# Two edge-maximum layers of a graph network: the attribute product and the gathered rows are summed in PSUM, and the maximum scan runs in four pieces

## The reference, cut to what matters

```
hv = x @ W_in + b_in
for W, b in ((W_u0, b_u0), (W_u1, b_u1)):
    m = concatenate([hv[src], he], axis=-1)     # he: 64 attributes of each edge
    m = relu(m @ W + b)
    msg = segment_max(m, dst)
    hv = where(has_in, msg + hv, hv)
out = relu(hv @ W_ro + b_ro)
```

## Time and profile before

| | |
|---|---|
| device time, median of 3 runs | 6830.46 us |
| the three runs | 6829.79, 6830.46, 6848.0 us |
| span of the profiled execution (one core) | 6822.1 us |
| mean granted TensorE clock over the span | 0.765 of full speed |
| TensorE busy over the span | 70% |
| VectorE busy over the span | 49% |
| GpSimd busy over the span | 48% |

### The profile page before, as it was taken

The page is one execution under the profiler, slowest core; times in us unless marked ns, Lnnn a source line. Parts: engine busy times, 40 slices in busy tenths (PEclk is TensorE's granted clock), DMA queues, the critical chain, the costliest instruction groups (busy, mean ns, idle before and its releaser), DMA issues. The chain is left out here.

```text
span 6822.1 us, 83340 instructions
## 1 busy us (share of the span) xinstructions
PE 4796.2 (70%) x21859; PEld 3705.9 (54%) x21860; DVE 3317.7 (49%) x8140; ACT 1583.2 (23%) x4023; POOL 3256.3 (48%) x2940
## 2 busy tenths in 40 slices
PE   3666576999844438699959566466567877688868
PEld 2666455677433326477759434244445666566645
DVE  5544467323433337622331466588434555355554
ACT  1000075333100008300014222265221111111121
POOL 2666677777566648300020444564325555555510
PEclk8555588999866769899969655598677777777778
DMA  4888655000288856376646344486436776577710
GB/s 131 271 265 272 189 191 168 8 1 1 62 279 283 276 191 235 120 250 219 195 158 211 113 139 138 148 311 232 138 119 176 203 200 196 158 202 202 204 61 24
DMA packets 751400, 1183.52 MB, mean 173 GB/s; under 512 B 100921, under 2 KB 528682, under 8 KB 750982
## 3 DMA queue, kind: packets, MB, share of 16 engines
q1 hardware_dynamic: 366758, 553.94, 26.0%
q0 software_dynamic: 135904, 356.79, 18.8%
q10 hardware_dynamic: 248448, 269.39, 11.7%
HBM read 818.22 MB, written 361.10 MB: 173 GB/s over the span
## 5 line engine op out<-in xcount | busy, mean ns | idle before, releaser
L2452 POOL DMA_INDIRECT max_rows<-tab,src_r x784 | 743.0, 948 | 607.1 <-DVE msg L2546 292.0
L403 POOL DMA_INDIRECT counts<-put_n,put_at x400 | 565.6, 1414 | 212.6 <-issue 134.8
L1009 POOL DMA_INDIRECT late_rows<-tab,src_a x416 | 418.4, 1006 | 317.7 <-DMA slot_rows<-late_rows 177.5
L2546 DVE TENSOR_TENSOR msg<-max_rows,ps_e 128x512 f32<-128x512 f32 x392 | 265.8, 687 | 557.3 <-PE ps_e L2483 158.2
L986 PE MATMUL ps_b<-q,sel_t 128*128 x832 | 277.8, 499 | 367.1 <-DVE sel_t L905 251.4
L707 POOL DMA_INDIRECT logit_rows<-tab,src_a x416 | 416.9, 1002 | 247.9 <-DVE logits L927 136.0
L707 POOL DMA_INDIRECT logit_rows<-tab_kv,src_a x416 | 396.8, 954 | 284.7 <-issue 125.1
L2483 PE MATMUL ps_e<-w,att 64*128 64x256 f32 x1568 | 515.1, 482 | 24.6 <-DMA att<-in_attr_t 17.2
L2558 DVE TENSOR_TENSOR_SCAN run<-same,run,ps_t 128x512 f32<-128x512 bf16 x392 | 479.4, 1265 | 9.8 <-remote 5.5
L2527 ACT ACTIVATE back<-ps_b 128x512 f32<-128x512 f32 x392 | 222.4, 596 | 1094.4 <-PE ps_b L2504 463.3
L826 PE MATMUL ps_a<-msg,sel 128*128 128x264 f32 (+1 forms) x1664 | 412.8, 397 | 90.2 <-DVEq L758 46.7
(11 more groups left out here) (482 smaller groups left out, 9786.7 us busy)
## 6 DMA issues: line engine op xcount, KB each, us to landing
blocks<-counts SPq DMA_DIRECT2D x390, 320.0 KB
slot_rows<-logit_rows ACTq DMA_DIRECT2D x208, 512.0 KB
edge_rows<-slot_rows SPq DMA_DIRECT2D x208, 512.0 KB
seg_rows<-back ACTq DMA_DIRECT2D x196, 512.0 KB
slot_rows<-late_rows SPq DMA_DIRECT2D x104, 512.0 KB
sum_rows<-slot_rows SPq DMA_DIRECT2D x104, 512.0 KB
counts<-zeros ACTq DMA_DIRECT2D x130, 320.0 KB
wf<-in_L_ffn_W SPq DMA_DIRECT2D x57, 512.0 KB
```

What stands on the lines that cost most here:

```text
L403: nc.gpsimd.indirect_dma_start(out=g.counts, out_offset=bass.IndirectOffsetOnAxis(ap=g.put_at[:, j:j + 1], axis=0), in_=g.put_n[:, j:j + 1 ...
L1009: self.nc.gpsimd.indirect_dma_start(out=self.rows[:, b * Q + j, :], out_offset=None, in_=self.g.tab, in_offset=bass.IndirectOffsetOnAxis(a ...
L2452: nc.gpsimd.indirect_dma_start(out=rows[:, b * Q + j, :], out_offset=None, in_=table, in_offset=bass.IndirectOffsetOnAxis(ap=g.src_r[:, n ...
L2546: v.tensor_tensor(msg[:, s:s + 2, :], rows[:, s:s + 2, :], ps_e[:, k, :].rearrange("p (j d) -> p j d", j=2), ALU.add).then_inc(mixed, 1)
```

## The change

In `edge_max` alone, and in one more host layout of the attributes:

- `att` of a group is one tile of 128 partitions: the attributes of the first 256 edges on partitions 0 to 63, those of the last 256 on 64 to 127. `w` is loaded twice, onto both halves of the partitions.
- `edges(n)` makes the product the other way around: `w` is stationary (64 rows by 128 features), `att` moves (256 edges), so features stand on partitions at once. Four products, two on each half of the array's rows, in turn, straight into `ps_t`.
- `turn(n)` no longer transposes `msg`: it multiplies each gathered 128x128 block (stationary) by the float32 identity (moving), as a product and not as a transpose, and accumulates onto what `edges` left in `ps_t`.
- `mix(n)`, `msg` and `ps_e` are gone. `ps_t` has a ring of three groups (`R`) in place of two.
- `scan(n)` is four scans of 256 columns in place of two of 512.
- GpSimd's gather of group n waits for turn(n-4) in place of mix(n-4), SP's load of `att` for edges(n-4).

```diff
--- before.py
+++ after.py
@@ -2423,31 +2423,31 @@
 def edge_max(nc, g, table, w_dram):
...
+    R = 3
+    HG = GP // 2
     with Phase(nc) as ph:
         sb, ps, sem = ph.sb, ph.ps, ph.sem
         rows = sb("max_rows", [P, W, D], F32)
-        w = sb("w", [EA, D], F32)
-        att = sb("att", [EA, W, P], F32)
+        w = sb("w", [2 * EA, D], F32)
+        att = sb("att", [2 * EA, Q, HG], F32)
         same = sb("same", [P, Q, GP], BF16)
-        msg = sb("msg", [P, W, D], F32)
         run = sb("run", [P, Q, KD, GP], F32)
         back = sb("back", [P, W, D], F32)
-        ps_e = ps("ps_e", [P, 2, 512])
-        ps_t = ps("ps_t", [P, 2, KD, 512])
+        ps_t = ps("ps_t", [P, R, 2, 512])
         ps_b = ps("ps_b", [P, 2, 512])
...
-                        pool.wait_ge(mixed, 2 * (n - Q) + 2)
+                        pool.wait_ge(turned, 2 * (n - Q) + 2)
...
-                sp.dma_start(w[:], w_dram).then_inc(w_in, 16)
+                for h in range(2):
+                    sp.dma_start(w[h * EA:(h + 1) * EA, :], w_dram).then_inc(w_in, 16)
                 for n in range(RG):
                     b = n % Q
                     if n >= Q:
-                        sp.wait_ge(made, 2 * (n - Q) + 2)
-                    sp.dma_start(att[:, b * Q:(b + 1) * Q, :], g.ins["attr_t"][n * Q:(n + 1) * Q, :, :].rearrange("r e l -> e r l")
-                                 ).then_inc(att_in[b], 16)
+                        sp.wait_ge(made, n - Q + 1)
+                    sp.dma_start(att[:, b, :], g.ins["attr_g"][n]).then_inc(att_in[b], 16)
                     if n >= Q:
-                        sp.wait_ge(ran, 2 * (n - Q) + 2)
+                        sp.wait_ge(ran, 4 * (n - Q) + 4)
                     sp.dma_start(same[:, b, :], g.same_rows[n * GP:(n + 1) * GP].partition_broadcast(P)).then_inc(same_in[b], 16)
...
                 def edges(n):
                     b = n % Q
                     pe.wait_ge(att_in[b], 16 * (n // Q) + 16)
-                    for k in range(2):
-                        if n:
-                            pe.wait_ge(mixed, 2 * (n - 1) + k + 1)
-                        for j in range(2):
-                            ins = t.matmul(ps_e[:, k, j * D:(j + 1) * D], att[:, b * Q + 2 * k + j, :], w[:], start=True, stop=True)
-                        ins.then_inc(made, 1)
+                    if n >= R:
+                        pe.wait_ge(ran, 4 * (n - R) + 4)
+                    for c in range(KD):
+                        for h in range(2):
+                            at = slice(h * EA, (h + 1) * EA)
+                            ins = t.matmul(ps_t[:, n % R, h, c * HG:(c + 1) * HG], w[at, c * P:(c + 1) * P], att[at, b, :], start=c == 0, stop=False)
+                    ins.then_inc(made, 1)
 
                 def turn(n):
                     b = n % Q
-                    if n >= 2:
-                        pe.wait_ge(ran, 2 * (n - 2) + 2)
-                    pe.wait_ge(mixed, 2 * n + 2)
-                    for c in range(KD):
-                        for j in range(Q):
-                            ins = t.transpose(ps_t[:, n % 2, c, j * P:(j + 1) * P], msg[:, b * Q + j, c * P:(c + 1) * P], g.ident[:])
+                    pe.wait_ge(got[b], 64 * (n // Q) + 64)
+                    for h in range(2):
+                        for c in range(KD):
+                            for j in range(2):
+                                at = c * HG + j * P
+                                ins = t.matmul(ps_t[:, n % R, h, at:at + P], rows[:, b * Q + 2 * h + j, c * P:(c + 1) * P], g.ident[:],
+                                               start=False, stop=c == KD - 1 and j == 1)
                         ins.then_inc(turned, 1)
...
                 def give_back(n):
                     b = n % Q
-                    pe.wait_ge(ran, 2 * n + 2)
+                    pe.wait_ge(ran, 4 * n + 4)
...
-                def mix(n):
-                    b = n % Q
-                    dve.wait_ge(got[b], 64 * (n // Q) + 64)
-                    if n >= Q:
-                        dve.wait_ge(turned, KD * (n - Q) + KD)
-                    for k in range(2):
-                        dve.wait_ge(made, 2 * n + k + 1)
-                        s = b * Q + 2 * k
-                        v.tensor_tensor(msg[:, s:s + 2, :], rows[:, s:s + 2, :],
-                                        ps_e[:, k, :].rearrange("p (j d) -> p j d", j=2), ALU.add).then_inc(mixed, 1)
-
                 def scan(n):
                     b = n % Q
                     dve.wait_ge(same_in[b], 16 * (n // Q) + 16)
                     if n >= Q:
                         dve.wait_ge(returned, 2 * (n - Q) + 2)
+                    dve.wait_ge(turned, 2 * n + 1)
                     for c in range(KD):
-                        dve.wait_ge(turned, KD * n + c + 1)
                         if n:
-                            dve.wait_ge(ran, KD * (n - 1) + c + 1)
-                        v.tensor_tensor_scan(run[:, b, c, :], same[:, b, :], ps_t[:, n % 2, c, :], run[:, (b - 1) % Q, c, GP - 1:GP],
-                                             ALU.mult, ALU.max).then_inc(ran, 1)
+                            dve.wait_ge(ran, 4 * (n - 1) + 2 + c + 1)
+                        v.tensor_tensor_scan(run[:, b, c, 0:HG], same[:, b, 0:HG], ps_t[:, n % R, 0, c * HG:(c + 1) * HG],
+                                             run[:, (b - 1) % Q, c, GP - 1:GP], ALU.mult, ALU.max).then_inc(ran, 1)
+                    dve.wait_ge(turned, 2 * n + 2)
+                    for c in range(KD):
+                        dve.wait_ge(ran, 4 * n + c + 1)
+                        v.tensor_tensor_scan(run[:, b, c, HG:GP], same[:, b, HG:GP], ps_t[:, n % R, 1, c * HG:(c + 1) * HG],
+                                             run[:, b, c, HG - 1:HG], ALU.mult, ALU.max).then_inc(ran, 1)
...
                 v.memset(run[:, Q - 1, :, :], 0.0).then_inc(zeroed, 1)
                 dve.wait_ge(zeroed, 1)
-                mix(0)
-                mix(1)
                 for n in range(RG):
                     scan(n)
-                    if n + 2 < RG:
-                        mix(n + 2)
 
...
+    ap["attr_g"] = ap["attr_t"].reshape(RG, 2, 2, EA, P).transpose(0, 1, 3, 2, 4).reshape(RG, 2 * EA, 2 * P)
```

More of the change, by code:

```diff
@@ L2441, in edge_max @@
         stored = [sem(f"stored{b}") for b in range(Q)]
-        w_in, zeroed, made, mixed, turned, ran, returned, taken = (sem(x) for x in (
-            "w_in", "zeroed", "made", "mixed", "turned", "ran", "returned", "taken"))
+        w_in, zeroed, made, turned, ran, returned, taken = (sem(x) for x in (
+            "w_in", "zeroed", "made", "turned", "ran", "returned", "taken"))
         with nc.Block() as block:
@@ L2462, in _ @@
                     if n >= Q:
-                        sp.wait_ge(made, 2 * (n - Q) + 2)
-                    sp.dma_start(att[:, b * Q:(b + 1) * Q, :], g.ins["attr_t"][n * Q:(n + 1) * Q, :, :].rearrange("r e l -> e r l")
-                                 ).then_inc(att_in[b], 16)
+                        sp.wait_ge(made, n - Q + 1)
+                    sp.dma_start(att[:, b, :], g.ins["attr_g"][n]).then_inc(att_in[b], 16)
                     if n >= Q:
-                        sp.wait_ge(ran, 2 * (n - Q) + 2)
+                        sp.wait_ge(ran, 4 * (n - Q) + 4)
                     sp.dma_start(same[:, b, :], g.same_rows[n * GP:(n + 1) * GP].partition_broadcast(P)).then_inc(same_in[b], 16)
-                sp.wait_ge(w_in, 16)
+                sp.wait_ge(w_in, 32)
             @block.tensor
@@ L2473, in _ @@
                 t = nc.tensor
-                pe.wait_ge(w_in, 16)
+                pe.wait_ge(w_in, 32)
                 def edges(n):
```

## The result

The changed kernel took 6715.37 us (median of four runs, 6708.18 to 6723.0), the kernel before 6831.03 us in the same rounds. The ratio is 0.9825, with a 95% interval from 0.9809 to 0.984. The profiled execution has a span of 6706.4 us, against 6822.1 us.

What follows compares the result with a forecast made beforehand. TensorE's chain at a changing clock plus stops was taken to bound edge_max (6.44 us a group). At 5.3 us a group 223 us, plus 20 behind the last gathers, go from 6822.1: 6579 us span, 6587 us median, range 6520 to 6910.

Steps and rivals of the forecast that it cites:

- The step that failed: In edge_max, a group without stops at full clock takes its largest term; 5.3 us taken in place of 6.44, saving 223 us.
- Rival 1: In edge_max, the clock rises but TensorE's stops stay: 4.82 + 1.37 = 6.19 us a group, 6761 us; chance 0.11.
- The argument against rival 1: From 3580 to 3785 us TensorE works 205 us in 205 us, so heavy product work alone brings no stops.
- the argument for the clock: Long stages of float32 products had clock 0.93 to 1.00; with two of three steps products, edge_max should reach 0.93 or more.
- GpSimd's floor of 4.95 us: GpSimd's time for a group's gathers in edge_max without waiting, gaps between gathers included: 4.95 us.
- The term for the DMA engines: DMA packets of an edge_max group, 4.77 us, need 5.54 us at a share of 0.86, 4.77 at 1.
- The 5.3 us: Forecast time of an edge_max group, taken between GpSimd's 4.95 and the DMA engines' 5.54 us.
- The price of edges: TensorE's eight edges records cost 1.92 us at full clock, as before; 0.96 at the least if the halves run side by side.
- The side sentence on the Trainium skill: By the skill's up to 2x, edges would take 0.96 us and TensorE's full-clock sum 3.86 us, leaving the forecast unmoved.
- Rival 3: In edge_max, the clock goes on alternating but the halves overlap: 6.44 to 6.76 us a group, 6830 to 6893 us; chance 0.14.
- scans of 256 columns: VectorE's four scans a group take 0.73 us each, 2.9 us together, hidden behind TensorE.
- The tail: Work behind each edge_max call's last gather falls from 19.3 to 9.5 us, saving 10 us a call, 20 in all.

Runs made afterwards that it cites:

- eight groups of room: The changed kernel with eight groups of gathered rows in the buffer in place of four: 6702.09 us, ratio 0.9874 to the kernel before.
- two groups ahead: The changed kernel with GpSimd gathering group n only after TensorE has turned group n-2 (n-4 before): 6702.33 us, ratio 0.988.
- three groups ahead: The changed kernel with GpSimd gathering at most three groups ahead of TensorE's turn in place of four: 6656.81 us, ratio 0.9809.
- clearing in between: The changed kernel with GpSimd clearing a 128x256 tile that nobody reads after every two gathers: 6678.44 us, ratio 0.9837.
- turn as transposes: The changed kernel with turn as eight transposes for sixteen product records, overwriting the attribute products: 6654.21 us, ratio 0.9806.
- The run without stops: The kernel before with GpSimd's gathers replaced by plain transfers of the same bytes from fixed rows: 6270.63 us, ratio 0.9243.

## Why the prediction was wrong

**The step that failed** is "At full clock without stops the group takes the largest of GpSimd's 4.95, TensorE's 4.82 and DMA". The stops were written down as a cost of 1.37 us with no known cause, and the forecast let them go together with the half clock. The clock did rise, to 0.90, and the stops stayed: 5.93 us a group in place of 5.3. (5.93 - 5.3) x 196 = 123 us, which is nearly all of the 127 us between 243 and 116. Rival 1, "The clock rises but the stops stay", was the right mechanism at a chance of 0.11, and gave 6761 us, 46 us too slow. That it came so near is in part luck, since both its terms were off and in opposite directions: TensorE needs 3.88 us in place of 4.82, and what the gathers add is 5.93 - 3.88 = 2.05 us in place of 1.37. The measured time lies inside the stated range, which the rivals had made wide.

**The argument against rival 1 failed too.** The stretch with 205 us of work in 205 us shows no stop, but GpSimd does nothing in it (0.00). It spoke of products and the stops belong to gathers. The row had both numbers. The same rows hold a stretch that the argument for the clock passed over, 2300 to 2490 us, with gathers, 80.56 us of TensorE's work in 190 us, and 0.68.

**GpSimd's floor of 4.95 us** was right as its own pace (1.25 us a gather: in the changed kernel eight follow each other at that) and wrong as a bound of the group. In the stretches around 5430 us seven kernels needed 1.46 to 1.50 us for each gather:

| kernel | gathers, time | us each |
|---|---|---|
| changed | 8 in 11.87 | 1.48 |
| eight groups of room | 8 in 11.75 | 1.47 |
| two groups ahead | 12 in 17.72 | 1.48 |
| three groups ahead | 8 in 11.71 | 1.46 |
| clearing in between | 8 in 11.80 | 1.48 |
| turn as transposes | 12 in 17.48 | 1.46 |
| three gathers a group | 9 in 13.49 | 1.50 |

From the first to the last gather of the first call it is 1.45 (transposes) to 1.49 us (three gathers), and 1.53 us with two groups ahead. Six of the seven have four gathers in a group and could not tell a cost of each gather from a cost of each group; the one with three can, with 4.50 us a group. Four gathers make 5.9 us. The kernel before was over that, at 6.44, most likely for its loop through VectorE; the change took it down to the pace of the gathers, where it stops paying.

**The term for the DMA engines**, 4.77 to 5.54 us, was no bound either: with plain transfers of the same bytes a group took 3.87 us at a share of 0.90. The gathers' own packets were never tried at that pace. The 5.3 us stood between two bounds of which neither held.

**The price of edges** was taken in full, 1.92 us. The halves overlap and it is 1.07 us. The side sentence on the Trainium skill ("TensorEngine Tiling (Array Packing)", Theoretical Speedup: up to 2x for a contraction of 64 or less) gave the better sum: 3.86 us by it, 3.88 measured with plain transfers; 4.82 in the prediction. That the two agree to 0.02 us is luck in part, since edges came out 0.11 us dearer than by the page's factor and turn 0.07 us cheaper than its row. The speedup of eight records is 1.99 / 1.14 = 1.75.

**Rival 3** ("the same, but the halves overlap") had this sum, 3.86 to 4.10, and its sentence that work only goes from VectorE to TensorE is what the runs with plain transfers show: 0.9254 and 0.9243. For the kernel as it is it was wrong, since the clock did not go on alternating at 0.75 and the group fell from 6.44 to 5.93.

**The clock.** "Two steps of three are products" was given as the reason for 0.93 or more. It was 0.90, and the kernel before, with its transposes, had 0.94 without stops. So the transposes alone did not bring 0.75; it took the stops as well. With stops the work did count: 0.92 with products in turn, 0.81 with transposes. The rule of the Trainium skill ("TensorE: Matmul & The Clock Gate", Part 4) that the full clock does not engage for transposes is not settled by this. The run without stops had 0.94 with transposes in 1.94 of each 3.86 us, but products filled the rest, as in the last 16 us of the call.

**Right:** scans of 256 columns (0.729 and 0.723 us; 0.73 predicted); turn's sixteen records at 1.95 us; the DMA bytes at nothing (a run with an eighth of the gathered bytes took the same time). That the third `ps_t` group is worth nothing no run shows. **The tail** went from 19.3 us to 5733.67 - 5717.85 = 15.8 us behind the last gather, not to 9.5: 3.5 us in place of 10 in the first call. Its landing of 4 us stood on no row; the last gather's packets ended at 5720.40, 2.6 us behind it, so what was mis-sized is the work after the landing, 13.2 us in place of 5.6. The rows:

```profile
5716.90 0.95 POOL L2452 DMA_INDIRECT max_rows<-tab,src_r  x1 [0.30 <-issue]
```

and the last store:

```profile
5733.30 0.37 ACTq L2531 DMA_DIRECT2D seg_rows<-back  x1
```

**What stays open** is why indirect transfers of GpSimd hold this stage to 1.47 us each. It is not GpSimd alone: the first 16 gathers of a call start 1.25 us apart with nothing between. It is not bytes, room, the wait of GpSimd, late rows, or one of the other transfers. Whether the indirect form or the scattered rows do it was not tried. That TensorE's reports come late beside them is seen in the trace; what delays them is not.

## What to carry to other kernels

A stop in which several engines wake together has a cause of its own: find it before costing a change of the work around it, by leaving out one transfer at a time. Here one run of the kernel before with plain transfers would have shown that 513 us hang on the gathers (6783.76 - 6270.63), and that the stage's own work was 3.86 us a group already. A stretch that shows no stop is evidence only if it holds the suspect; look at each engine's busy time in it, not only at the one that the change touches. To gain more here, the number of indirect transfers in a group must fall, as it did with three (0.9448) and with two (0.9282); nothing that was tried beside four of them moved their pace of 1.47 us for the better.

## What the runs showed of the hardware

- Indirect transfers from GpSimd came 1.45 to 1.53 us apart on average in this stage in the changed kernel and its variants with three or four of them in a group (1.61 in the kernel before), though GpSimd gives them out 1.25 us apart at the start of a call. Plain ones of the same bytes are free beside 3.87 us of TensorE's work (ratio 0.982 against 0.925 of the whole). 32 or 256 values of a row make no difference (0.9845).
- Beside them TensorE's reports of finished work came up to 6 us after the end of its records (5606.37 and 5612.55), five of them within 0.30 us. The rows that it needed had landed 8.2 us before the turn that reads them.
- Half clock can be a symptom: 0.74 to 0.75 with stops, 0.94 without, with the same instructions in TensorE. With stops, the work counted too (0.92 and 0.81).
- Products of contraction 64 on the two halves of the array overlap (1.99 to 1.14 us for eight records of 256 columns) in either order of issue.
